# Splitting queries and keys into bfloat16 parts: two of the three parts move from GpSimd to ScalarE, and the attention loops get fixed places and a marked return

## The chip, the cores and the metric

One Trainium2 chip, one core. The metric is the device time of one execution in microseconds (us). The kernel before takes 2246.19 us (median of 3 runs, 2245.32 to 2248.29).

## The reference, cut to what matters

Two transformer layers on x of 32 batches x 256 tokens x 128. Each layer normalises and modulates, runs attention with 16 heads of 8, adds the gated result, normalises again and runs a mixture of experts (top 2 of 8 in layer 0, top 1 in layer 1).

```python
q, k, v = (qkv[0], qkv[1], qkv[2])
scores = jnp.einsum('bhqd,bhkd->bhqk', q, k) / math.sqrt(Hd)
bias = -slopes[:, None, None] * rel
probs = jax.nn.softmax(scores + bias[None], axis=-1)
out = jnp.einsum('bhqk,bhkd->bhqd', probs, v)
...
scores = jnp.einsum('bhid,bhjd->bhij', q, k)
probs = jax.nn.softmax(scores / jnp.sqrt(jnp.float32(HIDDEN_DIM)), axis=-1)
```

The first form of attention is layer 0's, with a bias linear in the distance; the last two lines are layer 1's.

## The kernel before, in words

The program has five stages one after another: a setup, and for each layer an attention stage and an experts stage. Each is a block in which every engine has its own instruction stream; semaphores order them. The change touches the attention stage alone (and one constant of the setup).

**Scores in bfloat16 parts.** Queries and keys are projected in float32 (`project_qk`, L1101; ScalarE reads them into `qk`, `read_qk`, L688 to L699). For exact enough scores on TensorE in bfloat16 each value is split into three bfloat16 parts whose sum it is: part 0 is the value rounded, part 1 is the rounded rest, part 2 the rest of that. GpSimd does this in `split_qk` (L584 to L595) with four operations on 128 x 512 elements: L592 multiplies `qk` by a column of ones into part 0, L593 subtracts part 0 into `rem`, L594 multiplies `rem` by the ones into part 1, L595 subtracts part 1 from `rem` into part 2. Each waits for the one before it through the engine's own semaphore (`ch.link`).

**Stack.** SP (the queue of SyncE) copies the parts, in six copies for each half of the heads (`stack_up`, L514 to L522), into `stack`, where the products of parts lie one under another along the partitions, so that one product of TensorE sums them. `stack_max` (L524) adds the row maxima as two more rows.

**Two passes over the scores.** TensorE computes the scores of a head once in A (`scores_a`, L1114; L1122, with L1126 for the bias in layer 0), VectorE takes their row maxima (`row_max`, L863, L867), the negated maxima are split (`split_max`, L869, L874 and L875), turned and read by ScalarE (L713), and TensorE computes the scores again, with the maximum subtracted by the product itself, in B (`scores_b`, L1137; L1146 and L1149). ScalarE takes the exponentials, two heads at a time in eight chunks (`exps`, L715, L720), TensorE multiplies them with the values (`weigh`, L1153, L1161), ScalarE reads four heads' sums (`head_sums`, L723, L727), TensorE turns them back (L1169) and VectorE normalises (L889, L893). A has two buffers: head h of `scores_a` waits until the maximum of head h - 2 is taken. A head's first product in a half also waits for the stack's landing.

**Ticks.** One tick (`tick` of each engine) works on batches at different depth: maxima of batch i, exponentials of i - 1, the tail (routing of tokens to experts, the scatter of rows into `gathered`) of i - 2 and i - 3, and the projections and split of i + 1. The order within a tick is written out by hand for each engine. 38 ticks run; ticks -3 to 2 and the last ones are unrolled, 26 in the middle are 13 passes of a loop with two ticks each (`run_ticks`, L377 to L399, the loop at L389).

**GpSimd's tick** (L636): the split of i + 1; in layer 1 the product of the value weights with the gates (`gate_values`, L609); `modulate` of i - 2 (L616, L618); `scatter` of i - 3 (L629, indirect copies); in layer 1 `add_experts` (L602 to L604); and last `scatter_done`, which waits until the scatter has landed. So the next tick's split comes after that wait.

**ScalarE's tick** (L752): exponentials of chunk 0, the last head sums of i - 2, `second_h`, in layer 0 the first reciprocal root, chunk 1, `read_qk`, chunk 2, in layer 1 the first reciprocal root (L666, L667), `max_rows`, `head_sums` of group 0, chunk 3, `values` (L706), and so on to chunk 7 and `first_h`.

**VectorE's tick** (L1016): 16 maxima with the small operations between them. Those that the prediction speaks of: in layer 0 the choice of experts on the logits (`first_of`, L952: L954 to L958, called for the first and the second choice; L980 between them), `split_max` (L874, L875); in layer 1 `residual` (L916) and `outer_norm` (two L822).

**TensorE's tick** (L1193) holds among others the turn of the normalised heads `On` (L1092), which in layer 0 waits until ScalarE has read the values out of the same PSUM tile.

Of the kernel before, what the change touches and what calls it, by code (L numbers as in the profile page):

```python
# [122 lines left out]
def build(nc, a, out):  # L123
    with ExitStack() as ctx:
# [25 lines left out]
        ones_row = sb("ones_row", [1, P])  # L150
        ones_col = sb("ones_col", [P, 1, 1])
        rev_iota = sb("rev_iota", [P, 2, E])
# [122 lines left out]
        with nc.Block() as block:  # L275
# [40 lines left out]
            def _(dve):  # L316
# [11 lines left out]
                ch.mark(dve.memset(eps_col[:, 1:2], EPS_IN))  # L328
                ch.mark(dve.memset(ones_col[:, :, :], 1.0))
                for u in range(2):  # L330
# [44 lines left out]

def run_ticks(eng, tick, ch=None, per=0):  # L377

# [8 lines left out]
    if ch:  # L387
        ch.before()
    with eng.Fori(0, pairs) as k:  # L389
        if ch:  # L390
            ch.loop(k, 2 * per)
        for i in (DEPTH, DEPTH + 1):
            tick(lambda off: (k * 2 + (i + off), k + (i + off) // 2, (i + off) % 2))
        if ch:
            assert ch.n == 2 * per, ch.n
# [6 lines left out]
def attention(nc, l, g):  # L402
# [11 lines left out]
    gate_rows, ga_rows, wv_ga, wv_id = (g[n] for n in "gate_rows ga_rows wv_ga wv_id".split())  # L414
    gb_row, ones_col, Y, expert_out, XR, a, w1, w2, b1, b2 = (g[n] for n in
        "gb_row ones_col Y expert_out XR a w1 w2 b1 b2".split())
    n_choice = CHOICES[l]
# [13 lines left out]
    def transfers(name, dmas, begun=1):  # L431
# [25 lines left out]
                                        signal("pv", 4), signal("o_T", 4))  # L457
    split, h2_ready, scattered = signals("split", "h2_ready", "scattered")
    if l == 1:
        h3_ready = signal("h3_ready", 1)  # L460
        x2_ready, h_rows, base_ready, h_stats, h_rsqrt, rms_stats, rms_rsqrt, wv_ready = signals(
            "x2_ready", "h_rows", "base_ready", "h_stats", "h_rsqrt", "rms_stats", "rms_rsqrt", "wv_ready")
# [7 lines left out]
    with nc.Block() as block:  # L470
# [109 lines left out]
        def _(pool):  # L580
            start(pool, split, h2_ready, scattered, *([wv_ready, x2_ready] if l else []))
            ch = Chain(pool, pool_order)

            def split_qk(b, k, u):  # L584

                pool.wait_ge(qk_f32.handle, qk_f32.after(b))

                for half in range(2):
                    pool.wait_ge(stack_in[u][half], stack_in.of(k - 1))
                p = parts[u]  # L590
                one = ones_col[:, :, :].broadcast_to([P, 2, S])
                ch.link(pool.tensor_tensor(p[:, :, 0, :], qk[:, :, :], one, ALU.mult))  # L592
                ch.link(pool.tensor_tensor(rem[:, :, :], qk[:, :, :], p[:, :, 0, :], ALU.subtract))  # L593
                ch.link(pool.tensor_tensor(p[:, :, 1, :], rem[:, :, :], one, ALU.mult))  # L594
                pool.tensor_tensor(p[:, :, 2, :], rem[:, :, :], p[:, :, 1, :], ALU.subtract).then_inc(split.handle, 1)  # L595
# [55 lines left out]

            run_ticks(pool, tick, ch, 7 if l else 5)

        @block.scalar
        def _(act):
            start(act, rsqrt, h_ready, v_ready, onT_read, y_read, rsqrt2, h2T_read, w_exp, mT_read, b_exp, o_read, qk_f32)
            if l == 1:
# [30 lines left out]
            def read_qk(b, k, u):  # L688
# [6 lines left out]
                else:  # L695
                    ch.mark(act.activation(qk[:, 0, :], m[:, 0, :], ACT.Identity, bias=qs_bias[:, 0:1],
                                           scale=q_scale[:, 0:1]))
                    ins = act.activation(qk[:, 1, :], m[:, 1, :], ACT.Identity, bias=qk_bias[:, 1:2])  # L698
                ins.then_inc(qk_f32.handle, 1)  # L699

            def values(b, k, u):
# [50 lines left out]
            def tick(at):  # L752
# [16 lines left out]
                chunk(1)  # L769
                step(read_qk, 1)  # L770
                chunk(2)
                layer(1, first_rsqrt, 2)
                step(max_rows, -1, 1)
                step(head_sums, -1, 0)
                chunk(3)
                step(values, 0)
# [885 lines left out]
```

## Time and profile before

| | |
|---|---|
| median of 3 runs | 2246.19 us |
| the profiled execution | 2240.77 us, its span 2239.0 us |
| mean granted TensorE clock | 0.943 |
| busy: PE, PEld, DVE, ACT, POOL | 1779.3, 1283.3, 1652.0, 1039.1, 881.2 us |
| split on POOL: L592, L593, L594, L595, 64 of each | 66.5, 74.8, 68.7, 74.7 us |
| instruction queues over the whole span | q8: 28 packets, 0.46 MB; q14: 32 packets, 0.26 MB |

PE is TensorE's multiplication, PEld its weight load, DVE VectorE, ACT ScalarE, POOL GpSimd, SP the queue that issues most copies. A share of the span says little here, since the stages have different limits: the attention loops run from 137 to 724 us (layer 0) and from 1256 to 1876 us (layer 1), and the experts stages between and after them are not touched. The granted clock is 1.00 in layer 0's loop.

### The profile page before, as it was taken

To read this page: it belongs to the slowest core of one execution; us is meant where nothing else is said; L and a number is where in the kernel's file an instruction comes from. 1 tells how busy PE (TensorE), PEld (TensorE's weight loads), DVE (VectorE), ACT (ScalarE), POOL (GpSimd) and SP (SyncE) were. 2 spreads that over 40 slices of the span, in tenths; PEclk is the share of its full clock that TensorE was granted. 3 is DMA by queue.
4 is the path that set the end of the run, shared out by engine and by line. 5 is a ranking of instruction groups with operands and counts; after the bars stand their busy time and mean duration, and the time that the engine had idled before them with its cause. 6 is when DMAs were issued, how large, how long until landed. Compare 5 with 4: busy or idle time off the path is not lost. (4 is left out here: it accounts for less than half of the span.)

```text
span 2239.0 us, 57857 instructions
## 1 busy us (share of the span) xinstructions
PE 1779.3 (79%) x15650; PEld 1283.3 (57%) x15650; DVE 1652.0 (74%) x5861; ACT 1039.1 (46%) x1967; POOL 881.2 (39%) x932
## 2 busy tenths in 40 slices
PE   2599999999999947999935777777777878719997
PEld 1366666666666727999822444444444444417775
DVE  3488888888888855666626899899898888724453
ACT  0266666666666632222212555555555655603322
POOL 0224444444444333444423444444444444203333
PEclk9999999999999978999966999999999998959999
DMA  3343444343444323222235545545555454243332
GB/s 119 50 65 71 71 70 72 71 70 71 72 71 71 67 52 74 68 68 67 65 121 82 100 98 107 102 99 106 101 102 107 97 102 101 59 146 92 96 93 63
DMA packets 266022, 189.09 MB, mean 84 GB/s; under 512 B 25896, under 2 KB 256202, under 8 KB 265246
## 3 DMA queue, kind: packets, MB, share of 16 engines
q1 hardware_dynamic: 250602, 153.34, 34.7%
q0 software_dynamic: 15360, 35.03, 5.4%
q8 instruction: 28, 0.46, 0.1%
q14 instruction: 32, 0.26, 0.1%
HBM read 93.27 MB, written 53.18 MB: 65 GB/s over the span
## 5 line engine op out<-in xcount | busy, mean ns | idle before, releaser
L867 DVE TENSOR_REDUCE mx<-A 128x2 f32<-128x512 f32 x1024 | 691.8, 682 | 132.2 <-PE A L1126 52.8
L720 ACT ACTIVATE probs<-B 128x1024 f32<-128x1024 f32 x512 | 524.5, 1024 | 380.0 <-PE B L1146 195.5
L1122 PE MATMUL A<-stack 126*128 126x256 bf16 x2048 | 433.2, 283 | 136.2 <-DVE mx L867 102.5
L1146 PE MATMUL B<-stack 128*128 128x256 bf16 x2048 | 357.7, 277 | 32.6 <-DMA stack<-mrow 32.4
L1122 PEld LDWEIGHTS A<-stack 126*128 126x128 bf16 x2048 | 182.0, 99 | 296.8 <-DVE mx L867 213.9
L1161 PE MATMUL M<-probs,vals 128*32 128x256 f32 x4096 | 286.7, 396 | 22.0 <-DVE On L893 16.7
L629 POOL DMA_INDIRECT gathered<-h,slot_in x192 | 187.4, 976 | 154.4 <-DVE slot_in L1014 108.8
L1146 PEld LDWEIGHTS B<-stack 128*128 128x128 bf16 x2048 | 197.2, 101 | 84.3 <-issue 30.6
L616 POOL TENSOR_TENSOR h<-xn,back_rows 128x256 f32<-128x256 f32 x64 | 46.4, 726 | 498.9 <-DVE xn L822 498.9
L1562 PE MATMUL A<-w2s,hid 128*128 128x128 f32 x1792 | 230.4, 278 | 9.1 <-issue 9.1
L1562 PEld LDWEIGHTS A<-w2s,hid 128*128 128x128 f32 x1792 | 211.8, 192 | 18.4 <-issue 13.4
L1553 PE MATMUL B<-xtT,w1s 128*128 128x256 f32 x896 | 215.2, 393 | 5.3 <-DVE xtT L1439 2.0
L1368 POOL DMA_INDIRECT expert_out<-yt,row_dest x144 | 138.4, 961 | 175.4 <-DVE yt L1474 141.1
L1126 PE MATMUL A<-dist,slope_ident 128*128 128x128 bf16 x1024 | 200.6, 221 | 0.0
L1553 PEld LDWEIGHTS B<-xtT,w1s 128*128 128x128 f32 x896 | 167.4, 194 | 39.8 <-issue 16.4
L1161 PEld LDWEIGHTS M<-probs,vals 128*32 128x32 f32 x4096 | 124.9, 111 | 103.9 <-issue 33.9
L1149 PE MATMUL B<-dist,slope_ident 128*128 128x128 bf16 x1024 | 183.5, 219 | 0.0
L1522 ACT ACTIVATE hid<-B 128x1024 f32<-128x1024 f32 x72 | 73.8, 1024 | 226.6 <-PE B L1553 226.6
L592 POOL TENSOR_TENSOR parts<-qk,ones_col 128x512 bf16<-128x512 f32 x64 | 66.5, 1039 | 256.2 <-ACT qk L698 116.4
L1365 POOL DMA_INDIRECT out<-yt,row_dest x80 | 84.6, 1058 | 170.5 <-DVE yt L1479 147.0
L727 ACT ACTIVATE heads<-M 128x256 f32<-128x256 f32 x256 | 98.2, 384 | 106.3 <-PE M L1161 105.8
L1526 ACT ACTIVATE hid<-B,b 128x256 f32<-128x256 f32 x160 | 62.8, 475 | 174.0 <-PE B L1553 138.0
(192 smaller groups left out, 2980.0 us busy)
## 6 DMA issues: line engine op xcount, KB each, us to landing
stack<-parts SPq DMA_DIRECT2D x768, 64.0 KB
xt<-gathered SPq DMA_DIRECT2D x112, 132.0 KB, 2.2
probs<-gathered SPq DMA_DIRECT2D x40, 256.0 KB, 2.7
w<-in_w SPq DMA_DIRECT2D x4, 2048.0 KB
back_rows<-mod_rows SPq DMA_DIRECT2D x64, 128.0 KB, 3.3
x_mid<-X SPq DMA_DIRECT2D x64, 128.0 KB, 1.9
Y<-expert_out SPq DMA_DIRECT2D x64, 128.0 KB
X<-in_x SPq DMA_DIRECT2D x32, 128.0 KB, 3.0
```

What stands on the lines that cost most here:

```text
L629: pool.indirect_dma_start(gathered[l], bass.IndirectOffsetOnAxis(ap=slot_in[u][:, c, t:t + 1], axis=0), (h3 if l else h2)[u][:, t, :], Non ...
L720: act.activation(probs[c % 4][:, :, :, :], Bp[c % 2][:, :, :, :], ACT.Exp, scale=EXP_SCALE[l][c // 4]).then_inc(b_exp.handle, 1)
L727: act.activation(heads[g % 2][:, :], M1[:, 0:S], ACT.Copy).then_inc(o_read.handle, 1)
L867: dve.tensor_reduce(mx[u][:, h, :], A[h % 2][:, :, :], AX.X, ALU.max).then_inc(a_max.handle, 1)
L1122: ins = pe.matmul(A[h % 2][:, t, :], stack[u][0:n, h, 0, t * P:(t + 1) * P], stack[u][0:n, h, 1, :], start=True, stop=(l == 1))
L1126: ins = pe.matmul(A[h % 2][:, t, t * P:(t + 1) * P], slope_ident[:, h % HH, :], dist[:, t, :], start=False, stop=True)
L1146: ins = pe.matmul(Bp[c % 2][:, j, t, :], stack[u][:, h, 1, t * P:(t + 1) * P], stack[u][:, h, 0, :], start=True, stop=(l == 1))
L1149: ins = pe.matmul(Bp[c % 2][:, j, t, t * P:(t + 1) * P], slope_ident[:, h % HH, :], dist[:, 1 - t, :], start=False, stop=True)
L1161: ins = pe.matmul(M1[VW * j:VW * j + VW, 0:S], vals[u][:, t, 4 * g + j, :], probs[(2 * g + j // 2) % 4][:, j % 2, t, :], start=(t == 0), s ...
L1368: ins = pool.indirect_dma_start(expert_out[l], dest, yt[u][:, t, :], None)
L1553: ins = pe.matmul(dst[:, f, :], w1s[u][:, f * P:(f + 1) * P], xtT[u][:, :], start=True, stop=True)
L1562: ins = pe.matmul(A[u][:, t, 0:D], hid[u][:, f, t * P:(t + 1) * P], w2s[u][:, f, :], start=(f == 0), stop=(l == 0 and f == FC - 1))
```

## The change

Parts 0 and 1 are written by ScalarE as copies to bfloat16, `first_part` right behind `read_qk`, `second_part` between the head sums of group 0 and chunk 3. GpSimd keeps the two subtractions. Three semaphores order the four steps: part0 (ScalarE to GpSimd), part0_less (GpSimd to ScalarE), part1 (ScalarE to GpSimd). The wait for the stack's copies out of `parts` moves to ScalarE. The column of ones goes. The loop of `run_ticks` is opened for each engine with its first instruction at slot 0 of a fetch block and with a marked return: an instruction at the top of each pass announces the branch that closes it.

```diff
-                ch.mark(dve.memset(ones_col[:, :, :], 1.0))
...
+def loop_of(eng, rounds):
+
+    return eng.bass.Fori(0, rounds, engines=bass.OrderedEngineSet([eng.engine]), head_slot={eng.engine: 0},
+                         hint_back_edge=True)
...
-    with eng.Fori(0, pairs) as k:
+    with loop_of(eng, pairs) as k:
...
+    part0, part0_less, part1 = signals("part0", "part0_less", "part1")
...
             def split_qk(b, k, u):
 
-                pool.wait_ge(qk_f32.handle, qk_f32.after(b))
-
-                for half in range(2):
-                    pool.wait_ge(stack_in[u][half], stack_in.of(k - 1))
                 p = parts[u]
-                one = ones_col[:, :, :].broadcast_to([P, 2, S])
-                ch.link(pool.tensor_tensor(p[:, :, 0, :], qk[:, :, :], one, ALU.mult))
-                ch.link(pool.tensor_tensor(rem[:, :, :], qk[:, :, :], p[:, :, 0, :], ALU.subtract))
-                ch.link(pool.tensor_tensor(p[:, :, 1, :], rem[:, :, :], one, ALU.mult))
+                pool.wait_ge(part0.handle, part0.after(b))
+                pool.tensor_tensor(rem[:, :, :], qk[:, :, :], p[:, :, 0, :], ALU.subtract).then_inc(part0_less.handle, 1)
+                pool.wait_ge(part1.handle, part1.after(b))
                 pool.tensor_tensor(p[:, :, 2, :], rem[:, :, :], p[:, :, 1, :], ALU.subtract).then_inc(split.handle, 1)
...
-            run_ticks(pool, tick, ch, 7 if l else 5)
+            run_ticks(pool, tick, ch, 4 if l else 2)
...
+            def first_part(b, k, u):
+                for half in range(2):
+                    act.wait_ge(stack_in[u][half], stack_in.of(k - 1))
+                act.wait_ge(qk_f32.handle, qk_f32.after(b))
+                ch.settle()
+                act.activation(parts[u][:, :, 0, :], qk[:, :, :], ACT.Copy).then_inc(part0.handle, 1)
+
+            def second_part(b, k, u):
+                act.wait_ge(part0_less.handle, part0_less.after(b))
+                act.activation(parts[u][:, :, 1, :], rem[:, :, :], ACT.Copy).then_inc(part1.handle, 1)
...
                 step(read_qk, 1)
+                step(first_part, 1)
                 chunk(2)
                 layer(1, first_rsqrt, 2)
                 step(max_rows, -1, 1)
                 step(head_sums, -1, 0)
+                step(second_part, 1)
                 chunk(3)
```

## Rows read from the trace of the kernel before

In a timeline row: start in us, duration in us, engine, line, operation, what it writes and reads, shapes, count, and in brackets the idle time before it and what ended that.

**Rows 1.** Busy time by engine in ten passes of each layer's loop
```profile
228.70:678.80 450.10, 421.67 (x4620) 309.21 (x4620) 394.27 (x1322) 280.43 (x521) 195.93 (x200) 1.00 0.42 71
...
1351.60:1876.20 524.60, 407.19 (x3544) 240.17 (x3543) 468.72 (x1629) 306.50 (x617) 236.89 (x265) 0.95 0.51 103
```

**Rows 2.** Timeline of VectorE, layer 0, first tick of a pass and its end
```profile
598.26 0.17 DVE L955 TENSOR_TENSOR rt<-lg,r 128x16 f32<-128x16 f32 x1
...
598.88 0.70 DVE L958 TENSOR_TENSOR rt<-rev_iota,h 128x16 f32<-128x16 f32 x1
...
600.53 0.29 DVE L874 TENSOR_SCALAR mneg<-mx 128x16 bf16<-128x16 f32 x1
...
602.53 0.67 DVE L980 SCALAR_TENSOR_TENSOR rt<-rt,lg 128x16 f32<-128x16 f32 x1
...
611.16 0.68 DVE L867 TENSOR_REDUCE mx<-A 128x2 f32<-128x512 f32 x1
```

**Rows 3.** Timeline of VectorE, layer 0, second tick of the pass
```profile
620.58 0.96 DVE L955 TENSOR_TENSOR rt<-lg,r 128x16 f32<-128x16 f32 x1
...
621.98 0.82 DVE L958 TENSOR_TENSOR rt<-rev_iota,h 128x16 f32<-128x16 f32 x1
```

**Rows 4.** Timeline of GpSimd, layer 0, both ticks
```profile
598.52 1.03 POOL L592 TENSOR_TENSOR parts<-qk,ones_col 128x512 bf16<-128x512 f32 x1 [2.91 <-DMA gathered<-h,slot_in]
...
599.63 1.16 POOL L593 TENSOR_TENSOR rem<-qk,parts 128x512 f32<-128x512 f32 x1
...
602.01 1.16 POOL L595 TENSOR_TENSOR parts<-rem,parts 128x512 bf16<-128x512 f32 x1
...
620.47 1.04 POOL L592 TENSOR_TENSOR parts<-qk,ones_col 128x512 bf16<-128x512 f32 x1 [2.46 <-DMA gathered<-h,slot_in]
```

**Rows 5.** Timeline of TensorE matmuls, layer 0, first tick
```profile
600.91 0.44 PE L1092 MATMUL M<-ident,On 128*128 128x128 f32 x2 [0.32 <-ACT vals L706]
...
607.64 0.28 PE L1122 MATMUL A<-stack 126*128 126x256 bf16 x1 [0.37 <-DVE mx L867]
...
611.88 0.28 PE L1122 MATMUL A<-stack 126*128 126x256 bf16 x1 [0.77 <-DVE mx L867]
```

**Rows 6.** Timeline of ScalarE, layer 0, first tick
```profile
595.20 0.47 ACT L698 ACTIVATE qk<-M,qk_bias 128x256 f32<-128x256 f32 x1
...
598.51 0.39 ACT L727 ACTIVATE heads<-M 128x256 f32<-128x256 f32 x1 [0.18 <-PE M L1161]
...
599.56 1.02 ACT L720 ACTIVATE probs<-B 128x1024 f32<-128x1024 f32 x1 [0.67 <-PE B L1149]
```

**Rows 7.** Timeline of VectorE, layer 1, first tick and the loop's return
```profile
1590.37 0.17 DVE L874 TENSOR_SCALAR mneg<-mx 128x16 bf16<-128x16 f32 x1 [0.36 <-issue]
...
1597.29 1.40 DVE L916 TENSOR_TENSOR h<-On,xb 128x256 f32<-128x256 f32 x1
...
1600.49 1.10 DVE L822 TENSOR_SCALAR xn<-X,mv,rs 128x128 f32<-128x128 f32 x2
```

**Rows 8.** Timeline of ScalarE, layer 1, first tick
```profile
1595.53 0.38 ACT L694 ACTIVATE qk<-M 128x256 f32<-128x256 f32 x1
...
1598.88 0.39 ACT L727 ACTIVATE heads<-M 128x256 f32<-128x256 f32 x1
```

**Rows 9.** Timeline of GpSimd, layer 1, first tick
```profile
1599.67 1.16 POOL L595 TENSOR_TENSOR parts<-rem,parts 128x512 bf16<-128x512 f32 x1
...
1600.78 0.73 POOL L609 TENSOR_TENSOR wv_ga<-wv_id,ga_rows 128x256 f32<-128x256 f32 x1
```

**Rows 10.** Waits, 60 to 110 us, then 1184 to 1215 us: total, times, longest
```profile
PE A L1122 <- DMA stack<-parts: 18.7, 2, 13.1
...
PE A L1122 <- DMA stack<-parts: 6.6, 2, 5.6
```

**Rows 11.** DMA queues that moved anything between 184 and 728 us
```profile
q1 hardware_dynamic: 60506, 32.11, 36.0%
...
q0 software_dynamic: 3088, 6.53, 5.9%
```

More of the change, by code:

```diff
@@ L150, in build @@
         ones_row = sb("ones_row", [1, P])
-        ones_col = sb("ones_col", [P, 1, 1])
         rev_iota = sb("rev_iota", [P, 2, E])
@@ L414, in attention @@
     gate_rows, ga_rows, wv_ga, wv_id = (g[n] for n in "gate_rows ga_rows wv_ga wv_id".split())
-    gb_row, ones_col, Y, expert_out, XR, a, w1, w2, b1, b2 = (g[n] for n in
-        "gb_row ones_col Y expert_out XR a w1 w2 b1 b2".split())
+    gb_row, Y, expert_out, XR, a, w1, w2, b1, b2 = (g[n] for n in
+        "gb_row Y expert_out XR a w1 w2 b1 b2".split())
     n_choice = CHOICES[l]
@@ L580, in _ @@
         def _(pool):
-            start(pool, split, h2_ready, scattered, *([wv_ready, x2_ready] if l else []))
+            start(pool, split, part0_less, h2_ready, scattered, *([wv_ready, x2_ready] if l else []))
             ch = Chain(pool, pool_order)
             def split_qk(b, k, u):
-                pool.wait_ge(qk_f32.handle, qk_f32.after(b))
-                for half in range(2):
-                    pool.wait_ge(stack_in[u][half], stack_in.of(k - 1))
                 p = parts[u]
-                one = ones_col[:, :, :].broadcast_to([P, 2, S])
-                ch.link(pool.tensor_tensor(p[:, :, 0, :], qk[:, :, :], one, ALU.mult))
-                ch.link(pool.tensor_tensor(rem[:, :, :], qk[:, :, :], p[:, :, 0, :], ALU.subtract))
-                ch.link(pool.tensor_tensor(p[:, :, 1, :], rem[:, :, :], one, ALU.mult))
+                pool.wait_ge(part0.handle, part0.after(b))
+                pool.tensor_tensor(rem[:, :, :], qk[:, :, :], p[:, :, 0, :], ALU.subtract).then_inc(part0_less.handle, 1)
+                pool.wait_ge(part1.handle, part1.after(b))
                 pool.tensor_tensor(p[:, :, 2, :], rem[:, :, :], p[:, :, 1, :], ALU.subtract).then_inc(split.handle, 1)
@@ L650, in tick @@
                     scatter_done(*at(-3))
-            run_ticks(pool, tick, ch, 7 if l else 5)
+            run_ticks(pool, tick, ch, 4 if l else 2)
         @block.scalar
         def _(act):
-            start(act, rsqrt, h_ready, v_ready, onT_read, y_read, rsqrt2, h2T_read, w_exp, mT_read, b_exp, o_read, qk_f32)
+            start(act, rsqrt, h_ready, v_ready, onT_read, y_read, rsqrt2, h2T_read, w_exp, mT_read, b_exp, o_read, qk_f32, part0, part1)
             if l == 1:
```

## The prediction, written before the changed kernel was seen

> **What bounds the kernel now.** I read the busy time of ten passes of each layer's loop first. In layer 0 ten passes (two batches each) take 450.10 us, with TensorE busy 421.67 and VectorE 394.27; in layer 1 eleven take 524.60 us, with VectorE busy 468.72 and TensorE 407.19; ScalarE and GpSimd are busy 196 to 307 us [rows 1]. So two engines share the bound, and the time of GpSimd, which the change shortens, is no bound by itself.
>
> Then the timelines of one pass. In layer 0 TensorE waits for a row maximum (0.37 us at 607.64) although it is the busier engine [rows 5]: VectorE's chain of maxima and small operations runs without a wait for others from 598 us to the end of the tick, so what lengthens it there lengthens the tick. In this chain stand operations that take much too long: L955 takes 0.17 us at 598.26 but 0.96 at 620.58; L958 takes 0.70 and 0.82 on 16 elements a partition; L980 takes 0.67 [rows 2, 3]. Each of them ends 0.03 us after a split operation of GpSimd has ended: L958 at 599.58, L592 at 599.55; L980 at 603.20, L595 at 603.17; L955 at 621.54, L592 at 621.51 [rows 2 to 4]. So VectorE stands still while GpSimd works, if its operation reads two SBUF operands or is of some other forms. The split costs the kernel through these stalls.
>
> The Trainium skill (SBUF — State Buffer, "SBUF: two separate sides") says that VectorE and GpSimd share a port pair as an exclusive lock, held for a whole instruction by whichever starts first. By that rule what counts is when the remaining GpSimd operations run, and not that there are fewer; the trace agrees with the stall, 0.96 against 0.17 us. The rule speaks against a plain saving, and I follow the rows in the same way.
>
> **The change, part by part.** *Durations.* A ScalarE copy takes 0.39 us for 256 elements and exp takes 1.02 for 1024 [rows 6]; the line between them gives 0.60 for 512, so 1.2 us are added to ScalarE per batch. GpSimd loses L592 and L594 (1.03 us, and 1.06, which is what two handovers of 0.08 leave between 600.79 and 602.01) and keeps two subtractions of 1.16 [rows 4]. A handover costs 0.08 us (599.55 to 599.63) [rows 4]; the new chain has three more between engines.
>
> *Layer 0, first tick.* The first copy follows qk's end at 595.67 [rows 6] and is done at 596.3, in idle time of ScalarE. It cannot bring GpSimd forward: GpSimd is idle there for 2.91 us until its own scatter has landed, at 598.52 [rows 4]. The subtraction runs 598.52 to 599.68. ScalarE's next work is the second copy, placed after the head sums (end 598.90 [rows 6]); it waits for the subtraction and runs 599.76 to 600.36, and the second subtraction 600.44 to 601.60, against 603.17 before. On VectorE: L958 is held until 599.71 instead of 599.58, +0.13. L874, which ended at 600.82 [rows 2], would start at 600.66 and is held until about 601.63, so +0.81 in all. L980 then runs free, 0.17 instead of 0.67: +0.31 remains at the end of the tick.
>
> *Layer 0, second tick.* GpSimd comes at 620.47; L955 ends 0.14 later. ScalarE's copy runs 621.73 to 622.33, and L958, at 622.12, falls in the hole between the two subtractions and takes 0.17 instead of 0.82: -0.51. L874 behind it is held until 623.60, 0.3 earlier than before. The tick is 0.31 shorter. The two ticks cancel: 0 for layer 0's 13 passes. The ends of the range are both ticks like the second (26 x -0.31 = -8 us) and both like the first (+8).
>
> *The cover on ScalarE and TensorE.* ScalarE's exp of chunk 3 starts at 599.56 [rows 6]; behind the second copy it comes 0.8 later in the first tick, 0.45 in the second, and with it the values, for which TensorE already waits 0.32 us at 600.91 [rows 5]. I cost this at nothing because TensorE is ahead of VectorE later in the tick (the 0.37 us at 607.64); without that cover it is the slower rival below.
>
> *Stack transfers.* The split now ends 1.6 us earlier in layer 0, so SP issues the stack's copies earlier. TensorE idles 0.77 us before the first product of a tick (611.88) [rows 5]; the row names a maximum, but the only one that this product needs had ended before 611.16, so it is the stack's landing. The gain is nearly nothing: the second product needs the maximum that ends at 611.84 [rows 2], whatever lands.
>
> *Layer 1.* The first copy runs 1595.95 to 1596.55 behind qk (end 1595.91 [rows 8]), the first subtraction 1596.63 to 1597.79, so L916 (1.40 us at 1597.29 [rows 7]) ends up to 0.6 earlier. The head sums end at 1599.27 [rows 8]; the second copy is done at 1599.80 and the second subtraction runs 1599.88 to 1601.04, against 1600.83 before [rows 9]. The gates' product L609 follows on it, and the two L822, which end 0.08 after L609 now (1601.59 and 1601.51 [rows 7, 9]), end 0.21 later. The L916 gain is lost in that wait. In the second tick the head sums end 0.1 later against GpSimd, +0.31 by the same working. Mean 0.26, times 26 ticks in the loop: +7 us.
>
> *First batches.* With the pipeline empty, TensorE waits for the stack 13.1 us at longest in layer 0 (18.7 in two waits) and 5.6 in layer 1 (6.6 in two) [rows 10], behind the split. The split's chain was 4 operations, 4.7 us with handovers; it becomes 2 x 1.16 + 2 x 0.60 + 3 x 0.08 = 3.8 us. Five batches at -0.9: -4.5 us.
>
 One memset (ones_col) less in the setup: nothing.
>
> Sum: 0 + 7 - 4.5 + 1.3 = +4 us on the profiled 2240.8, that is 2244.8. The median of the runs is 5.4 above the profiled run, so 2250 by the median's measure. What a measurement of this kernel can tell from no change is about 0.2%, 4.5 us.
>
> **Rivals.** *A, VectorE wins the port in layer 1: faster.* With L916 out of the way VectorE reaches L822 between 1599.9 and 1600.5; GpSimd's second subtraction starts at 1599.88. The order is decided by a few tenths. If VectorE goes first, most of L916's gain stays and one hold drops out, 0.4 to 0.9 us a tick; at 0.65 x 26 = -17 us, with -4.5 and +1.3, the time is 2226. For it: the margin is small. Against: in the present rows GpSimd takes the port ahead of the second L822.
>
> *B, ScalarE becomes the late one: slower.* If TensorE's lateness at 600.91 is not made up, each tick of layer 0 pays the mean of 0.8 and 0.45, 0.6 us: 29 x 0.6 = +17, with +7, -4.5 and +1.3 gives 2267. It decides when the wait at 600.91 grows by more than the 0.37 us that TensorE has in hand at 607.64.
>
> *C, the loops' code.* A return that now fetches would become cheap, which would mean a gain; the rows show no fetch, 0.02. The reverse, a marked return that makes a fetch and stalls VectorE at 1 us or more in 26 passes, gives 2275 or more, 0.05. The Trainium skill (Runtime: NRT & Kernel Launch, "Instruction fetch mechanics") says that the non-TensorE engines hold two blocks of 256 instructions and that a jump out of them waits for a fetch; by it a badly placed loop of VectorE's length would fetch in each pass and the placement would save that. The trace shows no such fetch, so the rule changes only this small chance.
>
> **Chances.** Forecast 0.40, spread over 2240 to 2260; A 0.30, B 0.25, C 0.05. Slower by over 0.2%: B, the dear half of C and some 0.18 of the forecast, 0.45; within: 0.22; faster: A, the rest of C and a little of the forecast, 0.33. The range of 8 in 10 takes in A's and B's centres with their half widths: 2222 to 2272. The forecast's own range is 2240 to 2260.
>
> **What would show it.** In the changed profile: two ScalarE copies of 0.6 us; GpSimd's two subtractions with a hole of about 0.8 us between them; L980 at 0.17 in layer 0; L874 held up to 1 us in first ticks; L822's pair in layer 1 later or shorter, which separates A from the forecast; the wait for the values in TensorE's rows, which separates B; the wait for the stack at a tick's start gone in layer 0; no instruction queue in the loops. The forecast is wrong if layer 0's passes change by more than 0.6 us or layer 1's by more than 1.

## The result, and the profile after

The changed kernel takes 2261.2 us (median of 6 runs, 2257.5 to 2264.55), the kernel before 2245.76 us on the same chip (median of 6): ratio 1.0066, 95% interval 1.005 to 1.0082, that is +15 us. The profiled execution took 2263.73 us (span 2261.9), so in the two profiles the difference is 22.9 us. The profiled execution of before was a quick one of its kind, 5 us under its median; every difference by stretches below is taken against it, so their sums come out some 5 us too high, and no row says in which stretch. The range of 2222 to 2272 held the time. The point, 2250, was 11 us short, and the forecast's own part of the range, 2240 to 2260, was missed by 1 us.

First the page's busy times and code queues of the changed kernel (engine: busy us, share, instructions; queue: packets, MB):

```profile
PE 1792.3 (79%) x15650; PEld 1287.9 (57%) x15650; DVE 1658.6 (73%) x5860; ACT 1108.9 (49%) x2095; POOL 745.6 (33%) x804
...
q8 instruction: 29, 0.48, 0.1%
q14 instruction: 38, 0.31, 0.0%
```

POOL lost 135.6 us and ACT gained 69.8; DVE and PE, which bound the kernel, gained 6.6 and 13.0. The code queues carry one packet and six packets more than before (28 and 32). That is little code, but much of the time turns out to lie there.

To see where the time came, I took the start of ScalarE's read of `qk` (the second of its two) of each batch as a clock: one per tick. The spans between chosen batches, in us, and their differences to the kernel before:

```
stretch (start of qk's read, batch to batch)      before   changed    diff
start to batch 3 (first batches, layer 0)          123.4     119.5    -3.8
3 to 4 (layer 0's loop is entered)                  21.0      22.4    +1.3
4 to 29 (inside layer 0's loop)                    563.1     568.2    +5.1
29 to 31 (layer 0's loop is left)                   44.6      49.9    +5.3
31 to 32 (end of layer 0, its experts)             427.5     429.4    +1.9
32 to 35 (first batches, layer 1)                   60.3      56.7    -3.6
35 to 36 (layer 1's loop is entered)                22.1      24.2    +2.1
36 to 61 (inside layer 1's loop)                   596.1     602.2    +6.1
61 to 63 (layer 1's loop is left)                   47.8      54.9    +7.1
63 to the end                                      333.1     334.5    +1.4
```

The first batches give 7.4, the two loops take 11.2, entries and exits take 15.8, the rest 3.3: +22.9. The rest isn't followed up: the two stretches differ by 1 to 4 us from before in the experiments below too, on a chip like this one (once by 5.6). The forecast had -4.5, +7, and +1.3 for all that concerns the loops' code.

The timeline of VectorE, GpSimd and ScalarE in the changed kernel, layer 0, a first tick and the start of the second (start us, duration us, engine, line, operation, tiles, shapes, count, in brackets idle before and its releaser). They answer to [rows 2 to 4, 6]:

```profile
599.16 0.16 DVE L982 TENSOR_SCALAR h<-token_ids 128x2 f32 x1
...
599.42 1.00 DVE L968 TENSOR_TENSOR rt<-lg,r 128x16 f32<-128x16 f32 x1
600.87 0.17 DVE L971 TENSOR_TENSOR rt<-rev_iota,h 128x16 f32<-128x16 f32 x1
...
601.99 0.32 DVE L887 TENSOR_SCALAR mneg<-mx 128x16 bf16<-128x16 f32 x1
...
604.02 0.17 DVE L993 SCALAR_TENSOR_TENSOR rt<-rt,lg 128x16 f32<-128x16 f32 x1
...
621.34 0.86 DVE L982 TENSOR_SCALAR h<-token_ids 128x2 f32 x1
```
```profile
599.23 1.15 POOL L593 TENSOR_TENSOR rem<-qk,parts 128x512 f32<-128x512 f32 x1 [2.54 <-DMA gathered<-h,slot_in]
601.12 1.16 POOL L595 TENSOR_TENSOR parts<-rem,parts 128x512 bf16<-128x512 f32 x1 [0.74 <-ACT parts L710]
```
```profile
597.02 0.63 ACT L706 ACTIVATE parts<-qk 128x512 bf16<-128x512 f32 x1 [0.19 <-ACT qk L698]
...
600.42 0.63 ACT L710 ACTIVATE parts<-rem 128x512 bf16<-128x512 f32 x1 [0.36 <-POOL rem L593]
```

Line numbers moved: L954 to L958 are L967 to L971 now, L969 (the copy of the token numbers into the row) L982, L980 L993, L874 L887, L822 L835, L916 L929. The copies take 0.63, the hole between the subtractions is 0.74, and L993 runs free at 0.17: as forecast. By a hold I mean here that an operation of VectorE takes longer than when GpSimd is idle. In this tick it falls on L968 (1.00), because GpSimd starts while VectorE is at the head of this chain.

Then the place where layer 0's loop is left. TensorE's matmuls in the changed kernel, the granted clock around it (columns: window, length, busy us and count of PE, PEld, DVE, ACT, POOL, granted clock, DMA share, GB/s), and the code queue of 725 to 734 us:

```profile
730.35 0.37 PE L1135 MATMUL A<-stack 126*128 126x256 bf16 x1 [3.53 <-issue]
```
```profile
726.00:730.00 4.00, 0.81 (x9) 0.60 (x8) 2.72 (x9) 1.48 (x2) 2.57 (x4) 0.94 0.21 48
730.00:736.00 6.00, 5.65 (x39) 3.43 (x39) 2.02 (x6) 1.82 (x4) 2.79 (x3) 0.50 0.35 86
```
```profile
q8 instruction: 2, 0.03, 1.4%
```

TensorE stands for 3.53 us (726.8 to 730.35) and waits for nothing that the profile shows. Two packets of the code queue q8 pass in this stretch (16 KB each, at 727.5 and 732.4). The kernel before has one, at 728.9, and the next at 741.6. Behind the exit of layer 0 the first two stand 4.6 to 5.5 us apart in every kernel whose TensorE has the mark, and 11.6 to 17.4 us in all others, the one with the mark on all engines but TensorE among them: so I take q8 for TensorE's. Then TensorE runs 6 us at 0.50 of the clock, its lower level of 1.2 GHz, which adds to the price: in the kernel before the clock is 1.00 in both windows and the tick takes 22.5 us, here 28.35. At layer 1's exit the same:

```profile
1896.25 1.31 PE L1174 MATMUL M<-probs,vals 128*32 128x256 f32 x10 [2.71 <-issue]
```

In layer 1, the first tick in VectorE, GpSimd and ScalarE of the changed kernel, for [rows 7 to 9]:

```profile
1609.60 0.94 DVE L929 TENSOR_TENSOR h<-On,xb 128x256 f32<-128x256 f32 x1
1612.36 1.69 DVE L835 TENSOR_SCALAR xn<-X,mv,rs 128x128 f32<-128x128 f32 x2
```
```profile
1612.13 1.16 POOL L595 TENSOR_TENSOR parts<-rem,parts 128x512 bf16<-128x512 f32 x1 [1.87 <-ACT parts L710]
1613.25 0.72 POOL L609 TENSOR_TENSOR wv_ga<-wv_id,ga_rows 128x256 f32<-128x256 f32 x1
```
```profile
1611.15 0.39 ACT L738 ACTIVATE heads<-M 128x256 f32<-128x256 f32 x1
1611.43 0.62 ACT L710 ACTIVATE parts<-rem 128x512 bf16<-128x512 f32 x1
```

L929 got shorter by 0.46 (1.40 before), the pair L835 longer by 0.59 (1.10 before): it is caught behind the second subtraction and then behind the gates' product. The tick is 24.09 us on the mean of 22 ticks, against 23.84: +0.25, and 0.26 was forecast.

### The profile page after: what moved, and what is told of

It is laid out like the page before. It is cut to its first block and busy times, and to the rows that moved or that the text cites. A ratio compares the mean times of both kernels' runs of the same rounds, so it can differ in the third digit from the quotient of the medians.

```text
span 2261.9 us, 57910 instructions
## 1 busy us (share of the span) xinstructions
PE 1792.3 (79%) x15650; PEld 1287.9 (57%) x15650; DVE 1658.6 (73%) x5860; ACT 1108.9 (49%) x2095; POOL 745.6 (33%) x804
## 5 line engine op out<-in xcount | busy, mean ns | idle before, releaser
L1159 PE MATMUL B<-stack 128*128 128x256 bf16 x2048 | 363.0, 280 | 29.7 <-DMA stack<-mrow 29.5
L1174 PE MATMUL M<-probs,vals 128*32 128x256 f32 x4096 | 292.0, 401 | 24.0 <-DVE On L906 18.2
L593 POOL TENSOR_TENSOR rem<-qk,parts 128x512 f32<-128x512 f32 x64 | 74.0, 1157 | 282.1 <-ACT parts L706 223.7
```

Of the source, the lines that this page charges most:

```text
L1159: ins = pe.matmul(Bp[c % 2][:, j, t, :], stack[u][:, h, 1, t * P:(t + 1) * P], stack[u][:, h, 0, :], start=True, stop=(l == 1))
L1174: ins = pe.matmul(M1[VW * j:VW * j + VW, 0:S], vals[u][:, t, 4 * g + j, :], probs[(2 * g + j // 2) % 4][:, j % 2, t, :], start=(t == 0), s ...
```

## The experiments

They ran on three chips. On one the kernel before takes 2245.4 us, as on the first; on the two others 2377.8 and 2361.6. It was not profiled there, but the kernels that were have 88 to 120 us more in layer 0's loop than the kernel before on the first chip: their ticks take 26 to 28 us. I call this the stall. A stretch of such a tick, in the kernel with the loops' part alone (the windows' columns as above), and its waits from 240 to 800 us:

```profile
603.00:605.00 2.00, 0.62 (x8) 0.37 (x6) 0.18 (x1) 0.00 (x0) 1.40 (x2) 1.00 0.73 113
609.00:612.00 3.00, 3.00 (x20) 2.57 (x19) 1.90 (x5) 0.61 (x2) 2.19 (x2) 0.50 0.00 0
```
```profile
ACT heads L733 <- remote: 83.5, 20, 5.0
...
DVE mx L873 <- remote: 74.5, 21, 3.7
```

VectorE stops for 3.7 us and ScalarE for 5.0 at longest (3.5 and 4.2 on the mean) although the products they need are in the trace long before, and all go on together; then TensorE runs at half clock. Why these chips do it stays open: I found no transfer or instruction in the trace that accounts for it. Layer 1 and the first batches are the same on all chips to 1 us or so, so on the two slow ones I read only those, the entries and exits of layer 1, and how long VectorE's operations are held; ratios are against the kernel before on the same chip. They and the differences of the medians can disagree by up to 2.5 us, so each figure below says which it is where that matters.

**1. The split alone** (chip with the stall), and again on a chip without.

```
-    with loop_of(eng, pairs) as k:
+    with eng.Fori(0, pairs) as k:
```

> The split on ScalarE as in the changed kernel, the loops as before. Theory L (the loops' new entries and exits cost what the forecast missed, seen in the trace as some +1 to +2 us at each entry and +5 us at each exit): this kernel stands at the forecast without the marked return, +1 to +8 us on the kernel before, that is 2247 to 2254, with no tick of 28 us at the two exits and first batches 3 to 4 us shorter. Theory S (the split costs it, through ScalarE's and TensorE's lateness): it stands within 3 us of the changed kernel, 2258 to 2264.

> The split on ScalarE with the loops as before, once more. On a chip without the stall in layer 0's ticks: Theory L (loops cost it) +1 to +8 us on the kernel before, layer 0's passes within 0.6 us of before, layer 1's ticks +0.24. Theory S (the split costs it): +10 us or more. On a chip with the stall: -27 us again.

Measured with the stall: ratio 0.9886 (0.9869 to 0.9902), -27 us. Without: ratio 1.0031 (1.0021 to 1.0041), +7.0 us, or +7.9 by the medians; the profiled execution is +13.1 by span, some 5 of them the quick profile of before. By stretches, against the kernel before: first batches -4.8 and -4.7, entries 0, exits +0.6 and -0.8, layer 1's loop +6.2, layer 0's loop **+13.3**. So theory L has the time and the exits right and fails in layer 0, where it had the passes within 0.6 us of before and they are 1.06 longer: a tick there takes 23.09 instead of 22.51, while the changed kernel has 22.76. The place that I had taken for settled is the open one. The groups of VectorE in ten passes of layer 0 (228.7 to 678.8 us; count, busy us, mean ns, idle before), first the changed kernel, then the split alone:

```profile
L971 DVE TENSOR_TENSOR rt<-rev_iota,h 128x16 f32<-128x16 f32 x20 | 15.5, 775 | 0.7
L982 DVE TENSOR_SCALAR h<-token_ids 128x2 f32 x20 | 11.9, 596 | 0.0
L968 DVE TENSOR_TENSOR rt<-lg,r 128x16 f32<-128x16 f32 x20 | 9.8, 491 | 0.7
```
```profile
L971 DVE TENSOR_TENSOR rt<-rev_iota,h 128x16 f32<-128x16 f32 x20 | 23.5, 1174 | 0.7
L982 DVE TENSOR_SCALAR h<-token_ids 128x2 f32 x20 | 20.1, 1005 | 0.0
L968 DVE TENSOR_TENSOR rt<-lg,r 128x16 f32<-128x16 f32 x20 | 3.5, 175 | 0.7
```

Free they take 0.175, 0.16 and 0.175. Each tick of the split alone has two full holds, on L982 and L971.

**2. The changed kernel again**, beside it on the chip without the stall.

> The changed kernel itself, beside its halves on one chip. If nothing but the two parts of the change makes its time, it stands above the kernel with the split alone by what the placed and marked loops add to the kernel before: +10 to +14 us. On a chip whose layer 0 shows the stall of TensorE of 3 to 4 us in each tick (as the four kernels before this one), it is faster than the kernel before by 27 - 12 = 15 us; on one without the stall it is slower by 12 to 18 us.

Measured: ratio 1.0071 (1.0058 to 1.0084), +16.5 us by the medians: the result repeats. Layer 0's loop is +1.4 here by its profile (+5.1 in the first), with entries +1.3 and +0.5 and exits +5.3 and +8.7. It is 8.5 us over the split alone, under the +10 to +14 expected, since the loops' part takes 11.9 us back in layer 0's loop. How it does shows in the same first tick of the two kernels. The changed kernel:

```profile
596.68 0.16 DVE L982 TENSOR_SCALAR h<-token_ids 128x2 f32 x1
...
596.94 0.94 DVE L968 TENSOR_TENSOR rt<-lg,r 128x16 f32<-128x16 f32 x1
...
598.33 0.18 DVE L971 TENSOR_TENSOR rt<-rev_iota,h 128x16 f32<-128x16 f32 x1
```
```profile
596.70 1.15 POOL L593 TENSOR_TENSOR rem<-qk,parts 128x512 f32<-128x512 f32 x1 [2.49 <-DMA gathered<-h,slot_in]
598.59 1.15 POOL L595 TENSOR_TENSOR parts<-rem,parts 128x512 bf16<-128x512 f32 x1 [0.74 <-ACT parts L710]
```

And the split alone:

```profile
603.32 1.07 DVE L982 TENSOR_SCALAR h<-token_ids 128x2 f32 x1
...
604.49 0.17 DVE L968 TENSOR_TENSOR rt<-lg,r 128x16 f32<-128x16 f32 x1
...
605.12 1.18 DVE L971 TENSOR_TENSOR rt<-rev_iota,h 128x16 f32<-128x16 f32 x1
```
```profile
603.21 1.15 POOL L593 TENSOR_TENSOR rem<-qk,parts 128x512 f32<-128x512 f32 x1 [2.29 <-DMA gathered<-h,slot_in]
605.10 1.16 POOL L595 TENSOR_TENSOR parts<-rem,parts 128x512 bf16<-128x512 f32 x1 [0.74 <-ACT parts L710]
```

In the first, L982 starts 0.02 us before the first subtraction and runs; L968 is held 0.77, and L971 is over (598.51) 0.08 before the second subtraction starts. In the other, L982 comes 0.11 after the first subtraction and is held 0.91; all behind it is late by that, and L971 starts 0.02 after the second subtraction and is held 1.00. A tenth of a microsecond in GpSimd's start, which hangs on the landing of its scatter, makes 0.9 us a tick. In ten of the 11 first ticks of this stretch the changed kernel's subtraction starts 0.01 to 0.07 behind the copy, and in all 11 of the split alone 0.03 to 0.11 ahead of it. The difference is in GpSimd's wait: from the start of its last scatter instruction to the subtraction it takes 3.46 us on the mean here (3.48 in the first profile of the changed kernel) and 3.27 in the split alone. Why the loops' part makes this 0.2 longer is not shown. The Trainium skill (SBUF — State Buffer, "SBUF: two separate sides") puts it so that whoever starts first has the shared port pair for its whole instruction, and the other waits. For VectorE the trace agrees with that rule, 0.16 against 1.07 us for the same copy; GpSimd's subtraction takes 1.15 us in both cases, so that it ever waits for the copy doesn't show.

Over the 11 passes from batch 6 to 28, the tick against the sum of what its seven operations of this kind (the copy of the token numbers, the first choice, the maxima's split, L993) take beyond their free durations, in us:

```
                                first tick   held    second tick   held
kernel before                      22.35     1.27       22.66      1.49
changed kernel                     22.39     1.27       23.13      1.78
changed kernel again               22.23     1.11       23.03      1.77
split alone                        23.13     2.04       23.06      1.81
split, second copy early (3.)      23.11     2.03       23.04      1.80
```

The first tick follows the holds nearly one for one (0.90 us for 0.93 between the changed kernel again and the split alone). The second ones grow by 0.37 to 0.47 on the kernel before, for 0.28 to 0.32 more of holds.

**3. The second copy early.** ScalarE makes part 1 before its head sums; loops as before, no stall.

```
+                step(second_part, 1)
                 step(head_sums, -1, 0)
-                step(second_part, 1)
```

> Split on ScalarE, loops as before, and the second copy (part 1) ahead of the head sums in ScalarE's tick instead of behind them. Theory F (the forecast's: in layer 1 GpSimd's second subtraction holds the two normalisations of VectorE, and it comes late because the second copy waits behind the head sums): the second subtraction starts 0.4 us earlier, layer 1's ticks fall from +0.24 on before to 0 or under, -6 to -10 us against the split alone. Theory B (ScalarE and TensorE set the tick there): the head sums come 0.3 to 0.7 later and the ticks of both layers grow, +5 to +15 us against the split alone.

Measured: ratio 1.0007 (0.9998 to 1.0016), +3.1 us by the medians, so 4.9 less than the split alone, where 6 to 10 were expected. Layer 1's loop is +1.3 instead of +6.2, its tick 23.90 instead of 24.10. In GpSimd:

```profile
1582.32 1.16 POOL L595 TENSOR_TENSOR parts<-rem,parts 128x512 bf16<-128x512 f32 x1 [1.46 <-ACT parts L710]
```

The idle time before the second subtraction falls from 1.86 in the split alone to 1.46, and the pair L835 from 1.69 to 1.29. Theory F holds, with the smaller gain: it says why layer 1 lost time. Later head sums cost nothing that shows, against theory B. Layer 0 is as in 1., as it must be: there the second copy waits for the first subtraction in any case.

**4. The loops' part alone**, its two halves, and the mark without TensorE.

```
+def loop_of(eng, rounds):
+    return eng.bass.Fori(0, rounds, engines=bass.OrderedEngineSet([eng.engine]), head_slot={eng.engine: 0},
+                         hint_back_edge=True)
...
-    with eng.Fori(0, pairs) as k:
+    with loop_of(eng, pairs) as k:
```

For the place alone the last argument is left out, for the mark alone `head_slot`, and for the last kernel the mark is `hint_back_edge=eng.engine != mybir.EngineType.PE`.

> The kernel before, with the placed and marked loops alone. Theory L: +13 to +17 us on the kernel before, 2259 to 2263, with the ticks of 28 us at the exit of each layer's loop, and ticks inside the loops as before. Theory S: within 3 us of the kernel before.

> The kernel before, loops placed on a block boundary but without the mark. If the long tick at the exit belongs to the mark (what stands behind the loop isn't fetched while the loop runs), the exits are as before here (22.5 and 23.7 us ticks) and what is left is the entries, 0 to +4 us in all. If it belongs to the place (the code behind the loop then begins with a new block), the whole +13 to +17 us is here.

> The kernel before with the marked return but no placement. If the mark costs: +5 us at each exit, about +10 us in all, and no burst of instruction packets at the entries. If the placement costs: within 3 us of the kernel before. The forecast's price of the mark inside the loops, 0.1 us a pass, would be +1.3 us in each layer at most.

> The kernel before with the placed and marked loops, on a chip without the stall. Exits +5 and +6 us, entries +1 and +2, ticks in layer 1's loop +0.07, and in layer 0's loop between nothing and the +0.2 of the kernel with the mark on all but TensorE: +13 to +18 us in all. If the changed kernel's +16 is the sum of its halves (+7 for the split alone), this one stands at +9.

> The kernel before with the mark on the loops of all engines but TensorE, and no placement. If TensorE pays at the exits (its blocks are the larger ones, and its gap of 3.5 us stands in the changed kernel at 730 us), the exit ticks are as in the kernel before, within 2 us of it in all. If another engine's fetch is as dear, +4 us or more at each layer's exit remain.

The ratios, and the layer 1 stretches against the kernel before (us, from the profiles):

```
                              ratio    interval             entry   loop   exit
both (stall)                  1.0054   1.0040 to 1.0068      +0.2   +1.1   +6.5
both again (stall)            1.0098   1.0083 to 1.0114      +0.3   +1.7   +6.4
place alone (stall)           1.0009   0.9998 to 1.0020      +0.4   +1.4   -0.6
mark alone (stall)            1.0045   1.0029 to 1.0062       0.0   +0.2   +4.1
mark, not on TensorE          1.0076   1.0062 to 1.0090       0.0   +1.3   +4.1
```

The stretches are those of the table above (entry 35 to 36, loop 36 to 61, exit 61 to 63). So the exit belongs to the mark: without it there is none, with it 4 to 6.5 us. The entry belongs to the place. In layer 0 that is plain: +1.1 us in all three kernels with the place, 0 in the two without. The trace shows two things there. Each engine has one branch more at each loop (`COMPARE_BRANCH` at the loop's line: 28 an engine with the place, 26 without). And packets of the code queue q14 come in a burst, in every kernel with the place and in no other; in the changed kernel, between 132 and 140 us, where the kernel before has none:

```profile
q14 instruction: 6, 0.05, 2.0%
```

In layer 1 the entry is small and scattered: 0.2 to 0.4 with the place here, 2.1 and 0.5 in the two profiles of the changed kernel, -0.1 in 5. below. The totals on chips with the stall don't add up more closely than some 10 us (1.0054 and 1.0098 are one kernel on two chips), and the expected +13 to +18 was missed on both sides (+12 and +25 by the medians). The kernel with both never ran on a chip without the stall, so that its price there is the 8.5 us between the changed kernel and the split alone is not shown.

The kernel with the mark on all but TensorE, on the chip without the stall, was to be within 2 us of the kernel before if TensorE alone pays; it takes +17 (+18 by the medians). TensorE doesn't pay alone. By its profile layer 0's loop is +5.7 (holds 1.49 and 1.48 a tick; the second ticks are 0.23 longer than before with the holds as before, which stays open), its exit +2.8, the end of layer 0 +5.6, layer 1's exit +4.1. There VectorE stands:

```profile
1913.78 0.17 DVE L981 CAST sel<-rt 128x16 bf16<-128x16 f32 x1 [5.23 <-issue]
```
```profile
q14 instruction: 5, 0.04, 1.0%
q8 instruction: 1, 0.02, 0.4%
```

5.23 us in which it waits for nothing that the profile shows, with five packets of the other code queue (8 KB each) between 1900 and 1915 us, among 1876 data packets. The kernel with the mark alone, TensorE's too, has the same stop at the same place, and the same exit of +4.1:

```profile
2032.73 0.17 DVE L981 CAST sel<-rt 128x16 bf16<-128x16 f32 x1 [5.16 <-issue]
```

So at layer 1's exit TensorE's mark shows no cost by itself. TensorE's own stop stands there only in the kernels that have mark and place together (2.71 to 3.19 us, in four profiles), one tick earlier, and their exits are the dear ones of 6.4 to 8.7 us. Behind layer 1's exit all six profiles of kernels with a mark have stops of 1.9 to 5.2 us that nothing in the profile explains, on TensorE, VectorE or ScalarE; those without a mark have none above 1.3 us. For GpSimd no row shows one.

**5. Place without the mark, with the split** (stall).

```
-    return eng.bass.Fori(0, rounds, engines=bass.OrderedEngineSet([eng.engine]), head_slot={eng.engine: 0},
-                         hint_back_edge=True)
+    return eng.bass.Fori(0, rounds, engines=bass.OrderedEngineSet([eng.engine]), head_slot={eng.engine: 0})
```

> The changed kernel without the mark: split on ScalarE, loops placed. The exits are then as before. If the place of the code is what moves layer 0's ticks from 23.1 (split alone) to 22.6 on the mean (changed kernel): layer 0 at 22.6 and in all -2 to -4 us on the kernel before in layer 0, total +2 to +5 us. If the mark does it: layer 0's ticks at 23.1 and the total at +8 to +12 us.

Measured: ratio 0.9937 (0.9923 to 0.9951); the totals expected were those of a chip without the stall and can't be compared. Layer 1's exit is -0.5, its loop +5.9: the exit needs the mark with the split too. Whether the place moves layer 0's ticks from 23.1 to 22.6 can't be read on a chip with the stall, where GpSimd and VectorE meet otherwise: there the holds are 0.61 and 0.56 us a tick, as in the split alone on such a chip (0.60, 0.56), on one operation, the maxima's split. That stays open. The holds may be part of the -27 us of 1.: kernels with the split on GpSimd are held 1.0 to 1.7 us a tick on these chips. No run tests it, and the kernel before has no profile there.

**6. The copy of the token numbers moved away**, behind the second choice in layer 0: once with 3. and once in the kernel before (both with the stall).

```
             def choose_first(b, k, u):
-                ch.mark(dve.tensor_scalar(row[:, :, TOKEN], token_ids[:, bass.ds(b, 1), :].rearrange("p o t -> p (o t)"),
-                                          1.0, None, ALU.mult))
+                if l:
+                    copy_token(b, row)
...
                 dve.tensor_tensor(r1[:, 4, :], r1[:, 2, :], r1[:, 0, :], ALU.subtract).then_inc(w_den.handle, 1)
+                copy_token(b, h2[u])
```

`copy_token` holds the operation that is taken out in the first lines.

> Split on ScalarE with the early second copy and loops as before, and in layer 0 VectorE's copy of the token numbers (L982, held 0.99 us on the mean in layer 0's loop) moved behind the second choice, where GpSimd is idle. Theory P (the order in which VectorE and GpSimd start decides; here L982 starts a few hundredths after the first subtraction, and L971 a few hundredths after the second one): only L968 is held, until 0.77 us, L971 then ends before the second subtraction starts, and layer 0's ticks fall from 23.1 to 22.2 us, -20 to -26 us against the kernel with the early second copy alone, about 2225, faster than both kernels. Theory Q (TensorE, 21.1 us busy in each tick, or the values behind ScalarE, holds the tick near 23): within 5 us of that kernel.

> The kernel before with the same copy of the token numbers moved, the split on GpSimd. There it wasn't held (0.16 us), and L955, L958 and L980 are held 0.4, 0.6 and 0.25 us on the mean. Theory P: everything behind it in VectorE's chain comes 0.2 earlier, so the holds are as long or 0.2 longer, and the time is within 5 us of the kernel before. If it gains 10 us or more too, the gain of the kernel above isn't the split's.

Measured: ratio 0.9868 (0.9849 to 0.9887), -31 us (-29 by the medians), and 0.9991 (0.9981 to 1.0), -2 us. The first is the lowest ratio of all kernels here, but that of the split alone on the other chip with the stall is 0.9886, so the moved copy and the early second copy together are worth 0.2% with overlapping intervals there, and the 20 to 26 us expected don't show. Its holds did go:

```profile
L971 DVE TENSOR_TENSOR rt<-rev_iota,h 128x16 f32<-128x16 f32 x22 | 6.9, 312 | 0.8
L968 DVE TENSOR_TENSOR rt<-lg,r 128x16 f32<-128x16 f32 x22 | 3.8, 175 | 0.8
```

0.11 and 0.25 us a tick, against 0.60 and 0.56 of the split alone on such a chip, and the tick is 26.08 instead of 26.38. What it gives on a chip without the stall, where there are 2.03 and 1.80 us to take away, wasn't run. So between theories P and Q nothing is decided. The kernel before gains nothing from the move, as theory P has it: its holds are 1.67 and 1.02 a tick, no less than in the kernels with the copy in its old place on these chips (1.24 to 1.48 and 1.01 to 1.40), and fall on other operations of the choice.

## Why the prediction was right in its range and short in its point

**The range.** That 2222 to 2272 held the time is in part luck. Its upper end is there for rival B, centred on 2267, and B did not happen; what filled the room was the loops' code, for which the sum had 1.3 us and rival C 0.05. (C's two cases have 0.02 and 0.05 in its own paragraph, 0.05 together in the chances.)

**The bound** held in layer 0's first ticks: they follow VectorE's chain, 0.90 us for 0.93 us of holds.

**Durations.** The copies take 0.63 (0.60), the hole 0.74 (0.8): right.

**Layer 0, first tick.** +0.31 was forecast, +0.04 measured (-0.12 in the second profile). L993 runs free as said; the hold is on L968 and L887 and a little shorter.

**Layer 0, second tick.** -0.31 was forecast, +0.47 measured (+0.37). The step that failed is "GpSimd comes at 620.47; L955 ends 0.14 later": GpSimd comes sooner, and the first subtraction catches the operation ahead of those that I followed, the copy of the token numbers, which no row group had. In the kernel before it ran just ahead of the split; in the changed one the subtraction is 0.33 ahead of it:

```profile
620.31 0.16 DVE L969 TENSOR_SCALAR h<-token_ids 128x2 f32 x1
```
```profile
621.01 1.16 POOL L593 TENSOR_TENSOR rem<-qk,parts 128x512 f32<-128x512 f32 x1 [1.99 <-DMA gathered<-h,slot_in]
```

GpSimd's wait for its scatter, which I had left as it was (2.46 us [rows 4]), is 1.99 here. On the mean of 11 second ticks GpSimd takes 3.45 us from the start of its last scatter instruction to the split in the kernel before and 2.97 in the changed one (2.98 in its second profile, 3.00 in the split alone); the scatter lands 0.38 sooner and the split follows the landing 0.09 sooner. VectorE's way to the copy, from the slots that the same scatter waits for, stays at 10.37 and 10.39 us. So the order turns in every second tick. Why the scatter lands sooner isn't shown. The copy is held (0.86 at 621.34), the chain behind it is 0.7 late, and L971 doesn't fall into the hole but onto the second subtraction, held 1.00 where 0 was forecast. Over the 25 ticks of the stretch both kinds together give +5.1 us (+1.4 in the second profile) for the 0 that I wrote, inside the ends of -8 and +8. That both could be caught, as in the split alone, at +13.3, lay outside them: I had bounded by ticks that I had seen, not by each operation being caught once.

**ScalarE and TensorE, rival B.** TensorE's wait for the values grew from 0.32 to 0.54 us:

```profile
602.29 0.44 PE L1105 MATMUL M<-ident,On 128*128 128x128 f32 x2 [0.54 <-ACT vals L717]
612.91 0.28 PE L1135 MATMUL A<-stack 126*128 126x256 bf16 x1 [0.48 <-DVE mx L880]
```

0.22 more, less than the 0.37 in hand, and 0.40 against 0.33 on the mean of 20: B did not decide. The second row is the one at the stack's landing: the 0.77 before it [rows 5] are 0.48 now. In ten passes of the kernel before the waits for the stack are

```profile
PE A L1122 <- DMA stack<-parts: 3.4, 11, 0.7
```

and the changed kernel has none, as forecast.

**Layer 1.** +7 was forecast, +6.1 measured, by the mechanism forecast: experiment 3. moved the one cause and took 4.9 of it away (6.2 to 1.3 in the loop, 4.9 in all). Rival A (VectorE wins the port) did not happen: the pair L835 is longer, not shorter.

**First batches.** -4.5 was forecast, -7.4 measured. The waits for the stack that [rows 10] show:

```profile
PE A L1135 <- DMA stack<-parts: 16.4, 2, 11.9
...
PE A L1135 <- DMA stack<-parts: 5.8, 2, 5.2
```

They fell by 2.3 and 0.8 us in all; the rest of the gain is in waits that I had not counted, and the runs don't say in which.

**Loops.** This is the term that missed. For the entries it has "I take nothing", for the mark inside the loops "13 x 0.1 = 1.3 us". The loops' inside is right in layer 1 (a tick changes by 0.01 us with the mark alone, 0.05 with the place), and the extra instruction is there, once a pass and engine (`BRANCH_PREFETCH_HINT`, 130 in the trace). The entries cost 1.3 and 2.1, not nothing and at most 0.36 each, and the exits 5.3 and 7.1, which had no line in the sum at all. I had looked for code fetches in the running loop, found none [rows 11], and concluded that nothing was at stake; the rows at the exit itself, where fetching begins again, I did not ask for. Rival C named the code but put its price into the passes.
The sum as measured, by profiles: -7.4 first batches, +5.1 and +6.1 inside the loops, +3.4 entries, +12.4 exits, +3.3 elsewhere. By the medians the change costs 15.4 of these 22.9 us: the profile of before is 5 us under its median, that of the changed kernel 2.5 over its own. Without the loops' part (the split alone) the kernel is +7.9 by the medians, where the forecast without its 1.3 for the loops has +2.5. That this is near is luck too: its stretches are -9.5, +13.3 and +6.2 for the -4.5, 0 and +7 that I wrote.

## What to carry over

When code is put where it can be fetched better, ask for the rows at the loop's entry and exit, not in its passes: leaving a loop with a marked return cost 4 to 9 us in layer 1 and 3 to 5 in layer 0, and gained nothing in loops that fetched no code. Where VectorE and GpSimd share work in one tick, count the holds operation by operation, those ahead of the first held one too: on the chip without the stall fewer GpSimd operations didn't shorten the ticks, their places relative to VectorE's decided, and 0.1 us there was worth 0.9. Do not take the other engine's start for fixed either: it hung on a landing and a wait that the change itself shortened by 0.4 to 0.5 us. An operation with no urgent reader (here the copy of the token numbers) can go where the other engine is idle; it lost its holds there, but that this saves time was not shown.

## What was not expected of the hardware

A stop of TensorE of 3.5 us is followed by 6 us at a granted clock of 0.50, while ten passes of layer 0's loop before it run at 1.00. Chips differ: on two of them layer 0's ticks hold a common stop of VectorE and ScalarE of 3.5 and 4.2 us on the mean that the others don't have; the kernel before takes 5 to 6% longer on them, and the split alone made the kernel 0.3% slower on one chip and 1.1% faster on another. Its cause was not found.
